# Local attention in blocks of 32 queries, its mask laid by TensorE, on a skewed residual stream

## What is computed

```python
for i in range(6):                       # DEPTH
    x = attn_layer(shift_tokens(x), Wqkv[i], q_scale[i], k_scale[i], Wo[i]) + x
    x = ffn_layer(shift_tokens(x), ln_g[i], ln_b[i], W1[i], b1[i], W2[i], b2[i]) + x
# shift_tokens: the upper 64 channels come from the token before (zero at token 0)
# attn_layer: 16 heads of 64; q, k to unit length, times scale, rotary; then per block of
# WINDOW = 32 queries the 64 keys of its own and the previous block:
mask = (it < jb) | (it > jb + w) | (jb == -1)
sim  = where(mask, -max, einsum(bq, bk2) * 8);  attn = softmax(sim);  out = attn @ bv2
out @ Wo
# ffn_layer: layernorm(g, b) -> W1 (682 wide) + b1 -> a * gelu(gate) -> W2 + b2
```

## Time and profile before

| | us |
|---|---|
| three runs | 4344.21, 4346.10, 4350.79 |
| median | 4346.1 |
| span of the profiled execution | 4339.8 |

### The profile page before, as it was taken

One profiled execution on the slowest core, in us unless ns is written; L12 is line 12 of the kernel. 1 busy time (PEld: TensorE's weight loads), 2 busy tenths in 40 slices (PEclk: granted clock), 3 DMA queues, 4 the chain that ended last, 5 costly groups with the idle time before them and its releaser, 6 DMA issues. The chain is left out here.

```text
span 4339.8 us, 130231 instructions
## 1 busy us (share of the span) xinstructions
PE 3995.2 (92%) x46283; PEld 2655.5 (61%) x46283; DVE 3715.0 (86%) x12505; ACT 3380.3 (78%) x10657; POOL 3380.2 (78%) x4196
## 2 busy tenths in 40 slices
PE   6888799999999999999767999999999999996686
PEld 2333357767767767766553677767776776763464
DVE  6999789999999999999476999999999999974646
ACT  5888489999999999999414999999999999983122
POOL 3999698888888888888296888888888888861313
PEclk7999899999999999999897999999999999997887
DMA  1000101111111111111002111111111111100000
GB/s 28 1 1 1 46 24 31 41 31 36 41 27 49 31 34 44 26 34 27 15 1 53 31 27 41 36 41 31 36 41 27 51 29 29 37 24 3 6 3 10
DMA packets 78571, 122.04 MB, mean 28 GB/s; under 512 B 26024, under 2 KB 47204, under 8 KB 77924
## 3 DMA queue, kind: packets, MB, share of 16 engines
q1 hardware_dynamic: 77924, 113.71, 10.3%
HBM read 35.56 MB, written 1.05 MB: 8 GB/s over the span
## 5 line engine op out<-in xcount | busy, mean ns | idle before, releaser
L1095 POOL TENSOR_TENSOR local_qk<-local_qk,local_rb 128x512 f32<-128x512 f32 x768 | 975.7, 1271 | 224.2 <-DVE local_rb L1485 210.1
L1365 ACT ACTIVATE local_pr<-local_tb,local_nmax 128x96 f32<-128x96 f32 x3072 | 995.0, 362 | 68.7 <-DVE local_nmax L1501 67.1
L1191 PE MATMUL local_pj<-local_wqkv,local_xs 128*128 128x512 f32 x1536 | 808.4, 619 | 31.8 <-DVE local_rb L1485 17.8
L1101 POOL TENSOR_TENSOR local_qk<-local_qk,local_rinv 128x512 f32<-128x512 f32 x768 | 786.6, 1045 | 7.5
L1501 DVE CUSTOM_DVE_ANT_0 local_tb<-local_tb,local_mask 128x96 f32<-128x96 f32 x3072 | 689.2, 290 | 46.5 <-PE local_tb L1213 43.7
L1365 ACT ACTIVATION_READ_ACCUMULATOR local_pr<-local_tb,local_nmax 128x1 f32 x3072 | 703.3, 229 | 0.0
L1117 POOL TENSOR_TENSOR local_pr<-local_pr,local_rsum 128x384 f32<-128x384 f32 x768 | 622.4, 826 | 36.5 <-DVE local_rsum L1507 36.5
L1482 DVE TENSOR_TENSOR local_qk<-local_pj,local_rope 128x512 f32<-128x512 f32 x768 | 523.6, 682 | 62.8 <-ACT local_sq L1348 44.1
L1348 ACT ACTIVATE local_sq<-local_pj 128x512 f32<-128x512 f32 x768 | 462.2, 627 | 123.3 <-PE local_pj L1191 119.0
L1485 DVE TENSOR_TENSOR local_rb<-local_pj,local_rope 128x512 f32<-128x512 f32 x768 | 523.2, 681 | 2.8 <-POOL local_qk L1095 2.8
L1492 DVE TENSOR_REDUCE local_ss<-local_sq 128x8 f32<-128x512 f32 x768 | 512.0, 678 | 2.6 <-ACT local_sq L1348 0.8
(11 more groups left out here) (425 smaller groups left out, 7954.8 us busy)
## 6 DMA issues: line engine op xcount, KB each, us to landing
local_v<-local_v SPq DMA_DIRECT2D x288, 256.0 KB, 3.9
local_wqkv<-L_ffn_Wqkv_dram SPq DMA_DIRECT2D x72, 256.0 KB, 4.7
local_wo<-L_ffn_Wo_dram SPq DMA_DIRECT2D x12, 512.0 KB, 4.0
local_w<-L_ffn_W_dram SPq DMA_DIRECT2D x12, 341.0 KB, 4.8
mamba_parts<-mamba_in_low SPq DMA_DIRECT2D x24, 64.0 KB, 2.0
local_w<-L_ffn_W_dram SPq DMA_DIRECT2D x12, 128.0 KB
y_dram<-store_xtok SPq DMA_DIRECT2D x4, 256.0 KB, 2.9
local_oT<-rope_dram SPq DMA_DIRECT2D x2, 256.0 KB, 2.7
```

The costliest lines, as they stand in the source:

```text
L1095: nc.gpsimd.tensor_tensor(qk[:, u, :], qk[:, u, :], rb[:, u % 2, :], ALU.add).then_inc(s["summed"], 1)
L1101: nc.gpsimd.tensor_tensor(heads8(qk[:, u, :]), heads8(qk[:, u, :]), r, ALU.mult).then_inc(s["scaled"], 1)
L1191: nc.tensor.matmul(bank[:, :], xs[:, par, u // 4 * P:(u // 4 + 1) * P], wqkv[:, dep % 2, u % 4 * BANK:(u % 4 + 1) * BANK], start=True, sto ...
L1365: ins = nc.scalar.activation(pr[:, (NU * c + k) % PR_RING, i, WIN:WIN + KW], scores[:, i * KW:(i + 1) * KW], ACT.Exp, scale=-1.0, bias=nma ...
```

## The change

It does these things, in `local_transformer` and a little in `normalise`:

- **Blocks.** QB = 32: each block of 32 queries meets exactly its 64 keys (KW = 64). `score` has 2 calls (one per tile of 128 queries) of 64 matmuls of 64x32 weights and 64 columns. The mask (`maskb`, bfloat16) is laid into the two banks first by one 128x512 matmul each; the scores accumulate onto it. `maxima` becomes 4 plain VectorE maxima over 128x512. `exps` stays at 32, of 64 columns.
- **Values.** The probabilities are turned undivided: `turn_probs` has 2 calls of 16. `weigh` has 2 calls of 64 matmuls with the probabilities (64x32) as weights and 64 value columns, token-major, into a pair of `tb`. `scale_o` (VectorE, 4) divides while it evicts; the new `turn_o` (2 calls of 16 transposes) and `copy_o` (ScalarE, 4) bring the output back to channel-major. `norm_p` and the bank `ob` are gone; `ob`'s bank becomes `fa`, a second one for the feed-forward. `copy_v` goes from ScalarE to VectorE. `move_v` makes 8 transfers per item instead of 3.
- **Skewed stream.** z has L+1 columns, its upper 64 channels one column late, which is what `shift_tokens` wants. `shift_in` and the shifted sum in `residual1` are gone. `out_project` and `down` produce the skewed form: each matmul becomes two of 64 weight columns (one per half of the channels) and 257 columns. b2 becomes a row of w2.
- **LN root.** The ten `std` steps on VectorE and `spread_std` on ScalarE are gone: the two variances ride as two more columns in GpSimd's q/k root (ROOT_LEAD items ahead), and `spread_root` (GpSimd, one 128x256 product) makes the diagonals.
- **Order.** New lists for every engine, TAIL 5, down and up now at lag 5.

```diff
-QB = 64
+QB = 32
 KW = QB + WIN
-PAIRS_OF_BANKS = [("qk", 2, 2), ("probs", 3, 2), ("qk", 2, 3), ("probs", 3, 3), ("probs", 2, 0), ("score", 2, 1),
-         ("score", 2, 2), ("score", 2, 3), ("qk", 1, 0), ("qk", 1, 1), ("probs", 2, 1), ("score", 1, 0)]
+PAIRS_OF_BANKS = [("o", 4, 0), ("probs", 3, 0), ("qk", 2, 0), ("qk", 2, 1), ("o", 4, 1), ("qk", 2, 2),
+         ("score", 3, 1), ("weigh", 3, 0), ("probs", 3, 1), ("qk", 2, 3), ("score", 2, 0), ("weigh", 3, 1)]
+FREED = {"score": "exped", "probs": "probs_copied", "qk": "qk_copied", "weigh": "o_scaled", "o": "o_copied"}
...
+                if skewed:
+                    own = BANK // L
+                    for rows, first in ((slice(0, P // 2), 0), (slice(P // 2, P), 1)):
+                        nc.vector.tensor_tensor(net.skewed[rows, own * q:own * (q + 1), first:first + L], ...
...
+            def score(c, par, t):
+                sc = free_pair("score", c, t)
...
+                for h in range(2):
+                    nc.tensor.matmul(sc[h][:, :], net.identb[:, :], view(maskb[:, t, 0:1], [[0, PAIRS], [1, KW]]), start=True, stop=True)
+                pe.wait_ge(s["qk_copied"], QK_UNITS * c + 4 * t + 4)
+                for p in range(PAIRS):
+                    for i in range(BLOCKS):
+                        for h in range(2):
+                            own, q = slice(h * DH, (h + 1) * DH), t * P + i * QB
+                            ins = nc.tensor.matmul(sc[h][i * QB:(i + 1) * QB, p * KW:(p + 1) * KW], qT[own, par, p, q:q + QB],
+                                                   kT[own, par, p, q:q + KW], start=False, stop=True, skip_group_check=True)
...
+            def weigh(c, par, t):
+                ob = free_pair("weigh", c, t)
...
+                for p in range(PAIRS):
+                    for i in range(BLOCKS):
+                        for h in range(2):
+                            at = p * HALF + i % 2 * QB
+                            ins = nc.tensor.matmul(ob[h][i * QB:(i + 1) * QB, p * DH:(p + 1) * DH], prT[h * KW:(h + 1) * KW, t, i // 2, at:at + QB],
+                                                   window(par, BLOCKS * t + i, h)[:, p, :], start=True, stop=True)
...
             def out_project(e, par, part):
                 for j in range(4 * part, 4 * part + 4):
-                    ins = nc.tensor.matmul(fb[:, 0:L], wo[:, j, :], oT[:, j, :], start=(j == 0), stop=(j == INNER // P - 1))
+                    for h in range(2):
+                        own = slice(h * HALF, (h + 1) * HALF)
+                        ins = nc.tensor.matmul(fa[own, 0:L + 1], wo[:, j, own], oT[:, j, 1 - h:L + 2 - h], start=(j == 0), ...
...
             def iteration(run):        # TensorE's new list
+                run(turn_o, 4, 0)
+                run(spread, 5, 0)
+                run(project, 1, 1)
+                run(turn_probs, 3, 0)
+                run(turn_qk, 2, 0)
+                run(up, 5, 0)
+                run(up, 5, 1)
+                run(project, 1, 2)
...
+                run(score, 3, 1)
+                run(weigh, 3, 0)
+                run(down, 5, 0)
+                run(out_project, 4, 0)
+                run(out_project, 4, 1)
...
+                run(variance, 4, 0)
+                run(score, 2, 0)
+                run(project_v, 1, 0)
+                run(weigh, 3, 1)
+                run(project_v, 1, 1)
+                run(project_v, 1, 2)
+                run(project_v, 1, 3)
+                run(project, 0, 0)
...
+            def maxima(c, par, k):
+                nc.vector.tensor_reduce(nmax[:, t, h, :], pair_of_banks("score", t)[h][:, :].rearrange("p (a k) -> p a k", k=KW),
+                                        AX.X, ALU.max, negate=True).then_inc(s["maxed"], 1)
+            def scale_o(c, par, k):
+                nc.vector.tensor_tensor(o[:, t, :, h, :], heads8(pair_of_banks("weigh", t)[h][:, :]),
+                                        view(rsum[:, t, h, 0:1], [[1, PAIRS], [0, DH]]), ALU.mult).then_inc(s["o_scaled"], 1)
```

More of the change, by code:

```diff
@@ L1227, in weigh @@
[L1227 to L1240 removed]
+                    pe.wait_ge(s["mask_ok"], 1)
@@ L1275, in spread @@
                 pe.wait_ge(s["diag_ready"], e + 1)
-                for t in range(2):
-                    ins = nc.tensor.matmul(fb[:, t * P:(t + 1) * P], net.ones[:, :], diag[:, t, :], start=True, stop=True)
-                ins.then_inc(s["spread"], 1)
+                nc.tensor.matmul(fb[:, L:2 * L], net.ones[:, :], work[:, :], start=True, stop=True).then_inc(s["spread"], 1)
             def up(e, par, part):
@@ L1306, in iteration @@
+                run(turn_qk, 2, 1)
+                run(turn_o, 4, 1)
+                run(project, 1, 3)
+                run(up, 5, 2)
                 run(project, 1, 4)
                 run(turn_qk, 2, 2)
[L1308 to L1316 removed]
@@ L1317, in iteration @@
-                run(weigh, 3, 2)
-                run(turn_probs, 3, 3)
-                run(turn_probs, 2, 0)
-                run(up, 4, 1)
-                run(project_v, 2, 3)
-                run(score, 2, 1)
-                run(weigh, 3, 3)
-                run(score, 2, 2)
-                run(up, 4, 2)
-                run(project, 0, 0)
-                run(project, 0, 1)
-                run(down, 4, 0)
-                run(score, 2, 3)
-                run(turn_qk, 1, 0)
-                run(out_project, 3, 0)
@@ L1605, in iteration @@
-                run(copy_o, 3, 1)
-                run(affine, 4, 0)
+                run(rotate, 1, 2)
+                run(sum_squares, 1, 2)
+                run(gate, 5, 0)
+                run(gate, 5, 1)
+                run(gate, 5, 2)
+                run(maxima, 3, 2)
+                run(rotate, 1, 3)
+                run(scale_o, 3, 0)
+                run(maxima, 3, 3)
+                run(sum_squares, 1, 3)
+                run(rotate, 1, 4)
+                run(residual2, 5, 0)
+                run(scale_o, 3, 1)
```

660 lines of the change are left out of this document (288 added, 372 removed).

## The result

The kernel became slower: 4641.68 us (median, 4635.15 to 4648.46) against 4345.16 us of the kernel before on the same chip, a ratio of 1.068, 95% interval [1.066, 1.070]. The forecast was 4155 us, its range ended at 4300. The profiled execution took 4635.31 us, its span 4633.2.

A forecast was written before the change was run, and what follows sets the result against it. TensorE's list was taken as the bound: its terms sum to 30.44 us per item instead of 32.65, 198 us off over 90 periods, 5 on, giving 4155 us. The range ran from 4105 to 4300.

The forecast's parts named there:

- Values: again 16 groups of eight: 2 x (0.14 + 16 x 0.059) = 2.17 us: Values product (`weigh`) on TensorE, per item: two calls in eight tiles take 2.17 us, half of before (4.32).
- the scores: Score calls on TensorE: 2.21 us per item instead of 3.28, taking 0.059 us per group of eight, not 0.118.
- a group costs its columns plus a few ns, however many tiles share it: TensorE's small matmuls in scores and values: side-by-side tiles add no time; 0.0825 us per four, 0.059 per two.
- Rival B: Scores and values: small tiles do not run eight deep; gain lost at 0.093 us a group, 4495 us at four; chance 0.15.
- Rival C: Other late links (instruction supply, q/k scaling, a `pj` bank): 0.5 to 1.9 us per item given back, 4200 to 4325 us; chance 0.11.
- Out projection and `down`: TensorE, matmuls split into overlapping halves of 64 weight columns: 3.66 + 1.39 us per item, and 0.15 for changes of tiling.
- Mask: TensorE, four bfloat16 matmuls of 512 columns per item: 0.85 us and 0.2 for two changes of tiling, 1.05 us.
- Unchanged calls: TensorE's q/k/v projections, `turn_qk`, `centre`, `variance`, `up`: stay at 17.14 us per item, less 0.28 for fewer starts.
- Cover: VectorE, ScalarE and GpSimd all stay under 30.4 us per item, VectorE by least; `move_v`'s eight transfers are free.
- A: `turn_o` waits for its bank pair until the exps finish, or layernorm diagonals come late: 4215 us; chance 0.17.
- D: Whole kernel: the work moved equals the work saved, so no change, 4346 us; chance 0.03.
- if a segment of 128 lasts 2 us or more, B: Sign in the trace of score segments: 128 MATMULs near 1.6 us if right, 2 us or more means small tiles run slowly.

The follow-up runs named there:

- e1_nomove: Changed kernel with `move_v`'s eight transfers run for the first two sequences only, later items using those old values: 4641.23 us, ratio 1.068 to the kernel before.
- e1_bench: Changed kernel plus, behind each local stage, separate runs of small-tile and 4-column whole-array matmuls and short bursts; a burst of 256 instructions took 1.41 us, total not given.
- e2_even: Changed kernel with scores and values product each cut into quarters, long matmuls between, engine lists reordered: 4783.26 us, ratio 1.102 to the kernel before.

## Why the prediction was wrong

**Bound.** Right: TensorE's list is the time, and the other three engines stayed below it, at 25.3, 27.2 and 22.9 us against the 25, 27 and 23 named. What it did not ask is what TensorE itself needs besides data: its instructions.

**The step that failed** is "Values: again 16 groups of eight: 2 x (0.14 + 16 x 0.059) = 2.17 us": it puts the supply of instructions at nothing and the feed at the lower bound. It measured 5.59. 2.77 of the excess are gaps in the supply (two calls of 2.79 less two of 1.41). The remaining 0.65, and the 0.54 of the scores, are the feed: "a group costs its columns plus a few ns, however many tiles share it" held from two tiles to four, where the earlier trace rows had it, and no further. With eight tiles the 128 MATMULs of a call need 1.41 us, that is (1.41 - 0.15) / 16 = 0.079 us a group, since a load and a matmul together come every 11 ns. It lies between the two bounds of the text, 0.059 and 0.118, of which the lower was taken. The 5.2 us between forecast and result are thus 2.8 of gaps, 1.2 of feed, 0.8 in the unchanged calls and 0.5 in out projection and `down`, where the lower clock shows.

**Rival B** (slower side) placed it rightly in the groups of scores and values and gave 0.093 us as the point where all is lost. The feed alone came to 0.079, more than half way there. But its mechanism, tiles that do not run eight deep, did not happen; its 4495 us for four at a time is not how 4642 came about.

**Rival C** named the cause, "instruction supply in the densest stretch (a score and a values call back to back are 516 loads and matmuls in 2.3 us)", and gave it, among others, 0.5 to 1.9 us an item and 0.11. It was right about the place. The price was too small (2.8 us of gaps and 0.6 of clock), and it was taken as something given back from the gain. It could not be read from the kernel before, whose densest stretch, a score and a values call, has 128 loads and matmuls in 1.90 us, 256 in 3.8 at that pace, just clear of the limit. But the limit was asked for by nobody: for the new call pair the text had 516 of them in 2.3 us and no bound for what that could cost.

**Out projection and `down`**: right with 32 MATMULs in 3.58 us and 12 in 1.36 when undisturbed, 4.94 together for the 5.20 given. What lifts the mean to 5.69 is 0.15 of gaps that fell into them (4.4 us in the window) and 0.55 of clock: all ten falls began in `down` or just before it, and its 12 MATMULs then took up to 2.62 us, as at 1202.61 above. The prediction had no term for a clock below 1.00. **Mask** 1.06 for 1.05, `turn_*` 2.34 for 2.42, `spread` 0.54 for 0.53: right. **Unchanged calls** cost 0.84 more than given; 0.54 of it are the value projections (4.17 an item for 3.63 before), whose MATMULs last 640 ns where those of the queries last 612. Their weights are now read in pieces of 64 columns with gaps between. That does not make each MATMUL slower, for starts 0.42 us apart, the usual distance before, occur here too; distances of 0.5 us and more are only more frequent. The cause is open. **Cover**, `move_v` above all: right, e1_nomove shows that its eight transfers are free. **A** did not show: no wait of `turn_o` on PE in the window. **D** no.

The prediction's signs had "if a segment of 128 lasts 2 us or more, B". It did, and it was not B: whether MATMULs start evenly slowly or stop and go on had to be looked at.

## What to carry to other kernels

Count TensorE's instructions per time, not only its columns: here 256 loads and matmuls in less than about 3.5 us, in dense calls back to back, cost the difference as idle time put down to "issue". When a change cuts matmuls into smaller tiles, lay long matmuls between the dense calls, check that each call still stands clear of what it waits for, and price eight tiles by 11 ns for a load and a matmul. Look at the granted clock behind a gap before reading a slow call: what looks like a second gap can be half the clock. If idle time is put down to "issue", look for an instruction packet that lands 1.2 to 1.6 us before it ends, and add work in front of it, with a control elsewhere: if it is free only there, it is supply.

## What the runs showed that was not expected

- A block of 256 instructions of TensorE follows the one before in no less than 3.47 to 3.75 us (small tiles of e1_bench), at either clock: some 1.1 us to the start of its packet, 0.9 to 1.4 for the packet, 1.3 to 1.6 from its landing. Work that takes few instructions cost nothing in such gaps, 250 us of it here, in part because the clock then stayed up.
- Behind gaps of 1.8 to 2.6 us in an otherwise busy TensorE the granted clock fell to 0.50 ten times in 30 items of the changed kernel. In e2_even, where TensorE stood still longer (3.6 us an item) but for 1.2 us at a time at most, it did not fall.
- Matmuls in different tiles start without the 25 ns floor that the Trainium skill, TensorE: Matmul & The Clock Gate, section "Wait — 56ns, not 53.3ns?", gives. In one place the floor is there: over the whole array with 4 columns (e1_bench) MATMULs start 25.0 ns apart at the granted clock 1.00, 212 of them in 5.29 us, and 26.7 ns apart at 0.50, 465 in 12.44 us. In eight tiles it is 11 ns, and eight start within 0.05 us.
- The four times smaller volume of transfers in e1_nomove changed neither the time nor the gaps.
